# A graph network on one core: row gathers with a bound, fewer signals in the first layer, and a spacer of 200 columns

## The reference

```python
h = relu(layernorm(x))
x = x + gat(h)          # layer 0: scores a_src[src] + a_dst[dst], leaky ReLU, softmax over the edges of a node
h = relu(layernorm(x))
x = x + attention(h)    # layer 1: scores q[dst].k[src]/4 + edge_attr @ We + be, softmax, sum of v[src],
                        #          then Wo, residual and a layernorm with gain and offset
```

## Time and profile before

| | us |
|---|---|
| median of 3 runs | 1461.16 (1460.72 to 1461.55) |
| the profiled execution, its own time | 1460.96 |
| its span in the profile | 1459.2 |
| POOL busy | 1163.4 (80%) |
| PE busy | 933.9 (64%) |
| DVE busy | 922.7 (63%) |
| ACT busy | 636.4 (44%) |

### The profile page before, as it was taken

How to read it: one execution, slowest core, us unless ns; L and a number is a source line. 1 busy time by engine, 2 the same in 40 slices (tenths; PEclk the granted TensorE clock), 3 DMA queues, 4 the chain that set the end, 5 groups by cost and what they waited for, 6 DMA issues and landing times.

```text
span 1459.2 us, 21972 instructions
## 1 busy us (share of the span) xinstructions
PE 933.9 (64%) x4985; PEld 779.6 (53%) x4985; DVE 922.7 (63%) x3003; ACT 636.4 (44%) x1699; POOL 1163.4 (80%) x1806
## 2 busy tenths in 40 slices
PE   5546575756657576766475657675765767676574
PEld 4335464645545464555355546564654656565464
DVE  6546565656666666666843666665666666566668
ACT  5634344343434434341267353444445354444404
POOL 5888888888888888885138888888888888888810
PEclk9655656666565656655696787777778678677855
DMA  6332222222222222222133333333333333333301
GB/s 143 73 71 49 70 49 70 49 71 49 71 48 71 49 71 49 64 49 78 51 113 91 91 91 92 92 92 91 92 91 91 92 92 92 90 92 91 91 22 45
DMA packets 54209, 110.41 MB, mean 76 GB/s; under 512 B 16876, under 2 KB 30848, under 8 KB 53956
## 3 DMA queue, kind: packets, MB, share of 16 engines
q0 software_dynamic: 36288, 91.12, 23.9%
q1 hardware_dynamic: 16483, 17.39, 4.2%
q10 hardware_dynamic: 1313, 0.50, 0.1%
HBM read 100.60 MB, written 8.81 MB: 75 GB/s over the span
## 4 chain that ended last, share of the span: by engine, by line
POOL 77%; issue 11%; DVE 6%; PE 4%; ACT 1%; DMA 1%; DVEq 0%; POOLq 0%; SPq 0%; ACTq 0%
POOL G L512 57%; POOL pad_i L498 20%; PE bank L852 2%; DVE halves L1077 1%; ACT hn L566 1%; DVE acc L1438 1%; DVE mv L1084 0%; DMA G<-table,idx_all 0%; PE bank L750 0%; DVE G L1578 0%; DVE hn L1586 0%; DVE hn L1531 0%; DVE xs L1532 0%; DVE hn L1530 0%; PE bank L835 0%
## 5 line engine op out<-in xcount | busy, mean ns | idle before, releaser
L512 POOL DMA_INDIRECT G<-table,idx_all x880 | 843.6, 959 | 143.1 <-issue 111.3
L852 PE MATMUL bank<-PV,S 128*125 128x144 f32 x1760 | 427.8, 400 | 160.7 <-DVE PV L1411 141.2
L852 PEld LDWEIGHTS bank<-PV,S 128*125 128x125 f32 x1760 | 354.9, 274 | 189.8 <-issue 170.0
L1438 DVE TENSOR_TENSOR acc<-acc,bank 125x144 f32 x880 | 259.4, 295 | 138.2 <-PE bank L852 98.6
L498 POOL MEMSET pad_i<- 1x300 int32 x880 | 297.1, 338 | 18.0 <-DMA table<-h0b 9.3
L616 ACT ACTIVATE S<-iota_n,lid 128x125 f32<-128x125 f32 x880 | 275.7, 387 | 0.7 <-DVE pen L1172 0.7
L1411 DVE TENSOR_TENSOR PV<-G,bank 128x512 f32<-128x512 f32 x220 | 144.4, 678 | 35.1 <-issue 34.0
L629 ACT ACTIVATE ST<-bank 125x512 f32<-125x512 f32 x110 | 62.6, 596 | 232.3 <-PE bank L900 159.9
L620 ACT ACTIVATE S<-S,ones 128x500 f32<-128x500 f32 x220 | 156.6, 712 | 7.2
L835 PE MATMUL bank<-qe,ST 125*128 x880 | 139.8, 309 | 29.7 <-DVE prod L1229 29.2
L835 PEld LDWEIGHTS bank<-qe,ST 125*128 125x128 f32 x880 | 122.3, 215 | 40.3 <-issue 39.4
(11 more groups left out here) (221 smaller groups left out, 1215.7 us busy)
## 6 DMA issues: line engine op xcount, KB each, us to landing
G<-table,idx_all POOLq DMA_INDIRECT x880, 2.7
prod<-in_edge_attr_dram SPq DMA_DIRECT2D x8, 672.0 KB
table<-G SPq DMA_DIRECT2D x12, 224.0 KB
bias_rows<-qe SPq DMA_DIRECT2D x1, 1664.0 KB, 6.0
table<-h0b SPq DMA_DIRECT2D x8, 178.5 KB
out_dram<-G SPq DMA_DIRECT2D x8, 168.0 KB
prod<-in_edge_attr_dram SPq DMA_DIRECT2D x8, 90.0 KB
xs<-in_x_dram SPq DMA_DIRECT2D x1, 504.0 KB
```

The costliest lines, as they stand in the source:

```text
L512: pool.indirect_dma_start(G[:, u, v, 0:w], None, table, bass.IndirectOffsetOnAxis(ap=idx_all[:, g * GV + v:g * GV + v + 1], axis=0)).then_ ...
L852: last = pe.matmul(sums_bank(p)[0:BN, at:at + H * SLOT], S[:, ur, v, :], PV[:, v, :, :].rearrange("p h k -> p (h k)"), start=True, stop=True)
L1438: ve.tensor_tensor(a, a, o, ALU.add).then_inc(s.sem["acc_added"], 1)
```

## The change

The gathers get a bound: an index above 3124 is passed over and its row of `G` is left as it was, without an error. After the index tables are ready, DVE adds 4096 times the partition's number to the index of each foreign row, in all visits from the 49th on (groups 3 to 27), so that foreign rows lie above the bound, save those on partition 0. POOL waits for that before group 3. The spacer has 200 columns. In layer 0, three signals a group go (12 become 9): their waiters wait for signals of later PE work. PE does the transposes of the attributes before the fifth batch of sums, and DVE does `visit_scans` before `node_rows(2)`.

```diff
@@ -260,13 +260,14 @@
         s_ebfin = sem("bias_complete")
         s_out = sem("out_written")
         s_space = sem("spacer_set")
+        s_masked = sem("foreign_rows_masked")
         s_bias3 = sem("bias_parts")
         s_kvb, s_qmm, s_q, s_gain, s_res = (sem(n) for n in (
             "keys_values_complete", "queries_projected", "queries_complete", "gain_applied", "result"))
 
         NODE_SEMS = ("halves", "xc", "std", "inverse", "scales", "hn", "hT_ps", "hT", "feat", "feat_out", "feat_done")
 
-        LOOP_SEMS = dict(S_ready=QUARTERS, distances=QUARTERS, t_done=2 * GROUPS - 1, st_ready=QUARTERS, expanded=8, qk_done=0,
+        LOOP_SEMS = dict(S_ready=QUARTERS, distances=QUARTERS, t_done=GROUPS + 1, st_ready=QUARTERS, expanded=8, qk_done=0,
                          score_parts=GROUPS, scores_ready=GROUPS, es_ready=GROUPS, scoreT=GROUPS, esT_ready=GROUPS,
                          smax_ready=GROUPS, edge_scans=GROUPS, rh_ready=GROUPS, hop1=GROUPS, x_done=GROUPS,
                          carry=GROUPS, hop2=GROUPS, cc_mul=GROUPS, cc_done=GROUPS, f_done=GROUPS,
@@ -315,6 +316,20 @@
             else:
                 wait(eng, L[n]["mm_done"], sums_done(g - 2, (2, 3 if n else 2, 4, 4)[j]))
 
+        def wait_attr_product(eng, q):
+
+            if q > 0:
+                wait(eng, L[0]["mm_done"], sums_done(q - 1, 2))
+            else:
+                wait(eng, a_mm, q + 1)
+
+        def wait_attr_T(eng, g):
+
+            if g > 1:
+                wait(eng, L[0]["mm_done"], sums_done(g - 2, 4))
+            else:
+                wait(eng, a_T, g + 1)
+
         def transposed(n, g, j):
 
             return 2 * g + 1 + j // 2 + (n if g or j > 2 else 0)
@@ -382,7 +397,8 @@
             sp.wait_ge(s_lidout, 16)
 
             def load_ids(g, u):
-                wait(sp, L[0]["t_done"], transposed(0, g - UNROLL, 3))
+                wait(sp, L[0]["hop1"], g - UNROLL if g > UNROLL else 0)
+                wait(sp, L[0]["t_done"], 2 if g == UNROLL else 0)
                 sp.dma_start(lid_ring[32 * u:32 * u + 1, :],
                              lid_rows.rearrange("v e -> (v e)")[bass.ds(g * (GV * P), GV * P)].rearrange("(a c) -> a c", a=1)
                              ).then_inc(s_lid[u], 16)
@@ -399,7 +415,7 @@
                 if g % UNROLL or not has_attr(g, new):
                     return
                 ng = min(UNROLL, AG - g)
-                wait(sp, a_T, g)
+                wait_attr_T(sp, g - 1)
                 to = attr_in[:, 0:ng, :].rearrange("p u f -> p (u f)")
                 for lo, hi in ((0, 112), (112, 127)):
                     sp.dma_start(to[lo:hi, :],
@@ -503,15 +519,18 @@
 
                 for g in range(GROUPS):
                     u = g % UNROLL
+                    if n == 0 and g == UNROLL:
+                        pool.wait_ge(s_masked, 1)
                     for j in range(quarters(g)):
                         if n == 1 and g == UNROLL - 1 and j == 0:
                             pool.wait_ge(s_ebt, VK * H)
                         wait(pool, s["pv_ready"], 4 * (g - UNROLL) + j + 1)
                         for v in range(QV * j, QV * j + QV):
-                            space(300)
+                            space(200)
                             pool.indirect_dma_start(
                                 G[:, u, v, 0:w], None, table,
-                                bass.IndirectOffsetOnAxis(ap=idx_all[:, g * GV + v:g * GV + v + 1], axis=0)
+                                bass.IndirectOffsetOnAxis(ap=idx_all[:, g * GV + v:g * GV + v + 1], axis=0),
+                                bounds_check=NODES - 1, oob_is_err=False
                             ).then_inc(s_gath[u][j], 16)
 
             pool.wait_ge(s_idx0, 1)
@@ -657,13 +676,13 @@
                     if n and quarters(g + 1):
                         one_hot(g + 1, following, 0)
                     if n == 0 and mid and q < AG:
-                        wait(act, a_mm, q + 1)
+                        wait_attr_product(act, q)
                         act.activation(eb_nat[:, bass.ds(q * (ATTR_C * H), ATTR_C * H)], sm[:, 256:256 + ATTR_C * H],
                                        ACT.Copy).then_inc(a_out, 1)
                     if new:
                         if n == 0 and has_attr(g, new):
-                            wait(act, a_T, g + 1)
-                            wait(act, a_mm, g)
+                            wait_attr_T(act, g)
+                            wait_attr_product(act, g - 1)
                             act.activation(attrT[:, :], tp[0][:, :], ACT.Copy).then_inc(a_Te, 1)
                     if mid:
                         wait(act, s["al_mm"], q + 1)
@@ -811,7 +830,7 @@
                         wait(pe, a_Te, attr_done(g - 1))
                     last = pe.matmul(tp[j % 2][0:BN, :], ones_b[32 * u:32 * u + 1, :],
                                      lid_ring[32 * u:32 * u + 1, j * QV * P:(j + 1) * QV * P], start=True, stop=True)
-                    if j % 2:
+                    if j == 1 or (j == 3 and g == 0):
                         last.then_inc(s.sem["t_done"], 1)
 
                 def one_hot_T(g, u, j):
@@ -911,7 +930,8 @@
                         for k in range(QV):
                             last = pe.matmul(sm[:, 256 + 32 * k:256 + 32 * k + 32], attrT[:, k * P:k * P + P],
                                              WeBD[:, :, :].rearrange("p c h -> p (c h)"), start=True, stop=True)
-                        last.then_inc(a_mm, 1)
+                        if q == 0:
+                            last.then_inc(a_mm, 1)
                     if 3 * old > 4:
                         sums(g, u, 2)
                     if new > 3 and n:
@@ -924,14 +944,15 @@
                         expand(g, 2)
                     if new > 3:
                         expand(g, 3)
-                    if 3 * old > 8:
-                        sums(g, u, 4)
                     if n == 0 and has_attr(g, new):
                         pe.wait_ge(s_attr, 48 * (i + 1))
                         wait(pe, a_Te, g)
                         for k in range(QV):
                             last = pe.transpose(tp[0][:, k * P:k * P + P], attr_in[:, u, k * P:k * P + P], ident[:, :])
-                        last.then_inc(a_T, 1)
+                        if g < 2:
+                            last.then_inc(a_T, 1)
+                    if 3 * old > 8:
+                        sums(g, u, 4)
                     if mid:
 
                         wait(pe, s["p_ready"], q + 1)
@@ -1174,9 +1195,18 @@
             ve.wait_ge(s_vte, 8)
             ve.wait_ge(s_bz, 16)
 
+            foreign = PV[:, :, :, :].rearrange("p v h k -> p (v h k)")[:, 0:VISITS - UNROLL * GV]
+            later = slice(UNROLL * GV, VISITS)
+            ve.tensor_scalar(CC[:, 0:1], vcol_[:, 0:1], float(P * 32), None, op0=ALU.mult).then_inc(s_v, 1)
+            n_v[0] += 1
+            then(ve.tensor_scalar(foreign, lid[:, later], 0.0, float(BN - 1), op0=ALU.max, op1=ALU.min))
+            then(ve.tensor_tensor(foreign, foreign, lid[:, later], ALU.not_equal))
+            ve.scalar_tensor_tensor(idx_all[:, later], foreign, CC[:, 0:1], idx_all[:, later], op0=ALU.mult,
+                                    op1=ALU.add).then_inc(s_masked, 1)
+
             def bias_parts():
                 kv_rows = rowv[0:96, 2:4, :].rearrange("p k f -> p (k f)")
-                wait(ve, a_mm, AG)
+                wait_attr_product(ve, AG - 1)
                 then(ve.memset(bias3, 0.0))
                 then(ve.tensor_copy(bias_hi, kv_rows))
                 ve.tensor_copy(bias3[0:1, :], bias_hi[0:1, :]).then_inc(s_v, 1)
@@ -1214,7 +1244,10 @@
                     def node_rows(j):
                         if j >= new or n == 1:
                             return
-                        wait(ve, s["t_done"], transposed(0, g, j))
+                        if j < 2 or g == 0:
+                            wait(ve, s["t_done"], g + 1 + (g > 0 or j > 1))
+                        else:
+                            wait(ve, s["hop1"], g)
                         wait_expanded(ve, 0, g - 1, j)
                         ve.tensor_scalar(ST_b[:, QV * j:QV * j + QV, :],
                                          tp[j % 2][0:BN, :].rearrange("p (v e) -> p v e", v=QV), node, None,
@@ -1450,8 +1483,8 @@
                     edge_scans()
                     rescale()
                     edge_maxima()
+                    visit_scans()
                     node_rows(2)
-                    visit_scans()
                     add(0)
                     add(1)
                     carry()
```

## The result

| | before | after |
|---|---|---|
| median of 4 runs, us | 1460.94 (1460.03 to 1461.55) | 1442.15 (1440.49 to 1442.74) |
| profiled execution, its own time | 1460.96 | 1441.73 |
| its span | 1459.2 | 1440.0 |

The ratio of after to before is 0.9875, with an interval of 0.9862 to 0.9887: 18.8 us faster, where 71.7 were forecast. The change moves the lines of the file: the gather L512 is L530, its memset L498 is L514, the sums L852 are L871, `acc` L1438 is L1471, `raw` L1270 is L1303, `prod` L1229 is L1262.

The account below looks back on a forecast made before the run. POOL, running freely at a beat of 1.45 us for each gather and spacer, was taken to bound the kernel. 1461.2 less 71.7 for the shorter spacer, all other terms at nothing, gave 1389.5 us, range 1362 to 1470.

Parts of the forecast that it names:

- The spacer, 71.7 us: POOL's memset before each gather: 300 to 200 columns saves 0.0835 us on each of 859 gathers, 71.7 us.
- The bound, "I take 0": POOL's gathers: giving them a bound costs nothing, as a test of the index is likely already in the 952 ns.
- the two bounds, nothing and 78 ns: Cost of the bound per POOL gather: nothing if already tested, or 78 ns, the lower estimate from compare instructions.
- Rival C: POOL's gathers: the bound costs 78 to 199 ns each, break-even 83.5, ending at 1456 to 1560 us; slower, chance 0.19.
- a cheap C: POOL's gathers: the bound costs time but leaves part of the gain, 1410 to 1458 us; chance 0.12, shared with Rival B.
- Rival A: POOL's gathers at block boundaries: skipped rows shorten them, up to 43 us more, 1346 us; chance 0.10 beyond 10 us.
- Gathers of 544 and 1024 bytes take the same: POOL's gathers: medians of 951 and 952 ns at these row sizes, taken to speak for a fixed time.
- Rival B: Gathers can't be served faster for long and stretch as the spacer shrinks: 1425 to 1461 us; chance 0.12, shared with a cheap C.
- Landing times flat, DMA a third busy: Gather transfers: landings stay at 2.7 to 3.4 us, DMA engines 0.32 busy; taken against Rival B.
- Rival D: Compute takes over: PE's granted clock falls and a layer 1 step passes 21.8 us, 1408 us; inside the forecast's 0.54.
- Signals, order, masks, each at nothing: PE, ACT, DVE and SP: fewer signals, later waits, moved scans and DVE's masking, hidden behind gathers or left out, add nothing.
- The forecast that DVE's wait in layer 0 would fall to about 3.2 us from 4.6: Sign on DVE: its wait for gathers per layer 0 group shrinks so, as the beat falls to 1.36 us.

Follow-up runs that it names:

- e2: Kernel before with the spacer cut from 300 to 200 columns alone, first chip: 1391.08 us, ratio 0.9506.
- e6: Kernel before with the bound given and an index beyond it still an error (none is), second chip: 1527.55 us in one run, before there 1602.19.
- e1: Kernel before with the bound alone, no masking, spacer still 300 columns, first chip: 1516.05 us, ratio 1.0365.
- e3: Kernel after without its four masking instructions, a plain signal in their place, so every foreign row is fetched, first chip: 1443.46 us, ratio 0.9866.
- e4: Kernel before without any spacer, first chip: 1301.19 us, ratio 0.8896.
- e19: Kernel before with after's order and signals alone, spacer of 300 columns, no bound or masks, fifth chip: 1600.53 us, ratio 0.9991.
- e15: Kernel after without bound and masks, keeping its order, signals and spacer of 200 columns, fourth chip: 1840.05 us, ratio 1.1533.
- e16: Kernel before with the spacer of 200 columns alone, fourth chip: 1845.28 us, ratio 1.1543.
- e11: Kernel after, unchanged, on the third chip: 1701.52 us, ratio 1.0943 to before there.
- e14: Kernel before with a second memset of 2 columns after each spacer, fourth chip: 1599.75 us, ratio 1.0015.
- e5: Kernel after with the bound held in one register set once, in place of a move for each gather, second chip: 1773.94 us, ratio 1.1074.
- e7: Kernel after without any spacer, with bound, masks and order kept, second chip: 1945.8 us, ratio 1.213.

## Why the prediction was right and wrong

**The spacer, 71.7 us: right.** Measured alone it gave 71.7 (e2), by 83.5 ns on 859 gathers, as counted from the chain's share. The memset at 254 ns was right, and on that chip nothing else became late.

**The bound, "I take 0": wrong, and this is the step that failed.** It costs 50 ns on every gather, 859 x 0.050 = 43 us. The reason given was that the call before already treats an index beyond the table as an error, so that a test is in the 952 ns. The kernel with the bound and the error (e6) shows that this reason doesn't hold: a bound that is given costs 65 ns even so; whatever the call before tests, this test isn't in its 952 ns. The value lies between the two bounds, nothing and 78 ns, but the point was put on one end of them, though no row showed a gather that tests less. Rival C was thus the right mechanism, with its break-even of 83.5 ns rightly placed; its price lay below its own lower end. The stretch in which the result fell (1410 to 1458, "a cheap C") had a chance of 0.12. The rule on branching in the Trainium skill, GPSIMD Engine Reference, section Performance versus the Vector engine, would have put 1.28 us on each gather, as an estimate; no run shows it, and the 50 ns are the same whether rows are passed over or not.

**A term that was missing.** The bound, written as a number, also brings a register move for each gather. It is hidden, but it makes three instructions a gather, and in after and e1 POOL then stops for 0.99 us once in 73: 11 us. No row of before showed this, and the change names no such instruction, but "what does this call turn into" was never asked. With it the sum is 71.7 - 43 - 11 = 17.7 us, against 18.8 measured. The register version, which has no stops, wasn't run on the first chip; the 11 us are read from the traces.

**Rival A: wrong**, by e3. "Gathers of 544 and 1024 bytes take the same" was the right row to argue from: the gather's time doesn't go by what it fetches. The Trainium skill, DMA: Bandwidth & Descriptors, section on the anatomy of a software-generated DMA, calls the generation of descriptors small and variable. Here POOL is busy for 952 ns with each of 880 gathers, which sets the time of the kernel, and minimum and median are 2 ns apart: neither small nor variable by these rows.

**Rival B: wrong where the result was measured; elsewhere the spacer was there for a reason, but not for B's.** Its mechanism was put as gathers that stretch. They stretch nowhere (956 ns on the fourth chip, 952 without a spacer on the first). What goes late is what PE reports to DVE and ACT, and it does so on four of the five chips of the experiments, where the change lost up to 9.4% and the shorter spacer alone 15.4%; B had allowed at most that the whole gain goes. "Landing times flat, DMA a third busy" was no evidence on that, since neither is the thing that suffers. Four gathers in a row were also too few to show it, as the prediction itself said.

**Rival D: did not come.** The kernel after still hangs on POOL, at a mean granted clock of 0.688 where it was 0.693, and with no spacer at all (e4) the clock was 0.725.

**Signals, order, masks, each at nothing: right**, by e19, by e15 beside e16, by e3, and by the sum of e1 and e2. The forecast that DVE's wait in layer 0 would fall to about 3.2 us from 4.6 was as wrong as the beat: it fell by 0.8, with 16 x 0.036 = 0.6 us to come from a beat of 1.41.

**What stays open**: what differs between the chips, whether it is the chip at all and not its state at the time (each was used for one set of runs only), and how the late arrival works. It goes with closely spaced gathers; nothing in the DMA records stands out, as the packets of the gathers' queue took the kernel before as long on the one side (23.9% of its span of 1459.2 us, 349) as on the other (22.4% of 1545.2, 346, on the third chip). Nor is it known what stops POOL. The leave to pass rows over, without a bound of its own, wasn't tried alone, nor were beats between 1.45 and 1.51 us or longer than 1.59. No version was found that beats both kernels on all five chips. On the first, the spacer of 200 columns alone does (1391.08 us), and no spacer more so (1301.19).

## What to carry to other kernels

Where an engine that issues runs freely, its beat is the sum of all that it does for each piece, and a convenience in the call (a bound, a number that must first go into a register) is paid on every piece; measure the call alone before it is paired with a gain. A delay between transfers that looks like waste may stand for a limit that one profile doesn't show: run the version without it on more than one chip, and look at who waits "remote", not at the transfers. Where the same kernel's time differs between chips, compare only with the kernel before on the same chip.

## What was not expected of the hardware

- An indirect DMA of 128 rows costs POOL 952 ns, 1004 with a bound that passes rows over and 1017 with one that is an error, whatever is fetched or left out (544 or 1024 bytes a row; with 5% of the rows passed over or with none).
- With three instructions for each gather (e1, e3, e6, e11, e14, after) POOL stopped for 1 us once in 73 gathers; with a memset and a gather (before, e2, e5) it never did. With a move and a gather at a shorter beat (e7) it stopped nine times. The queue that the profile calls "instruction" moved 87 packets in after and 79 before, but 77 in e7, and at 8 of the 11 stops of after the trace has no packet of it from 3 us before to the end of the stop. So its count doesn't explain the stops. Below it is the line of after, and that of the kernel before on the third chip:

```profile
q14 instruction: 87, 0.70, 0.2%
```
```profile
q14 instruction: 79, 0.65, 0.1%
```

- On four of the five chips of the experiments the kernel before took 1551 to 1604 us instead of 1461 to 1463, and a shorter beat made it slower still: on the third 1551 at 1.45 us, 1702 at 1.41 and 1909 at 1.25; on the fourth 1596 at 1.45, 1600 at 1.59, 1845 at 1.36. In the place shown, a signal of PE reached DVE 6.6 us late while gathers were being issued.
